# A fused gated cross-attention and ternary feed-forward layer: opening reordered, loads split over two queues, unread matmuls at more waits

## The reference

```python
def reference(x, ctx, g_xattn, g_ffn, Wk, Wv, bv, Wq, bq, Wo, bo, w1, conv_w, conv_b, w2):
    # x [8, 100, 512], ctx [8, 722, 512], Wq/Wk/Wv/Wo [512, 512], w1 [2048, 512], w2 [512, 2048]
    q = layernorm(x) @ Wq.T + bq
    k, v = ctx @ Wk.T, ctx @ Wv.T + bv
    p = softmax(q @ k.T / sqrt(512))
    x = x + tanh(g_xattn[0]) * ((p @ v) @ Wo.T + bo)
    # feed-forward: rows quantised to int8 steps, weights to -1, 0, 1 times their mean magnitude
    h = quant_rows(layernorm(x)) @ ternary(w1).T
    h = silu(conv1d over the 100 positions, 3 taps per hidden channel, + conv_b)
    return x + tanh(g_ffn[0]) * (quant_rows(h) @ ternary(w2).T)
```

## Time and profile before

| | us |
|---|---|
| median of 3 runs | 359.85 (353.22, 359.85, 360.3) |
| the profiled execution | 355.76 |
| its span | 353.9 |
| TensorE busy in the span | 293.7 (83%) |
| VectorE, ScalarE, GpSimd busy | 184.7, 154.0, 99.5 |
| mean granted TensorE clock | 0.923 of 2.4 GHz |

### The profile page before, as it was taken

One profiled execution on the slowest core, in us unless ns is written; L12 is line 12 of the kernel. 1 busy time (PEld: TensorE's weight loads), 2 busy tenths in 40 slices (PEclk: granted clock), 3 DMA queues, 4 the chain that ended last, 5 costly groups with the idle time before them and its releaser, 6 DMA issues.

```text
span 353.9 us, 4349 instructions
## 1 busy us (share of the span) xinstructions
PE 293.7 (83%) x1565; PEld 206.8 (58%) x1565; DVE 184.7 (52%) x390; ACT 154.0 (44%) x255; POOL 99.5 (28%) x96
## 2 busy tenths in 40 slices
PE   4957999989988989758988996776978897868695
PEld 2427899656536766537767784544836854434342
DVE  0094232330225127577577347489857545897562
ACT  3003228684367552588541234198731102976000
POOL 1008000024210980234214003053420802544070
PEclk9995599999999999985999998799988589999899
DMA  6998139806696259500240600000000000000002
GB/s 194 235 247 342 53 110 272 192 1 154 159 417 152 60 119 252 142 0 3 74 95 5 164 2 0 0 3 23 2 23 0 0 0 25 1 24 25 0 0 69
DMA packets 27950, 32.19 MB, mean 91 GB/s; under 512 B 17865, under 2 KB 17865, under 8 KB 26778
## 3 DMA queue, kind: packets, MB, share of 16 engines
q1 hardware_dynamic: 27930, 31.93, 33.0%
HBM read 26.09 MB, written 1.64 MB: 78 GB/s over the span
## 4 chain that ended last, share of the span: by engine, by line
PE 22%; DVE 15%; issue 12%; ACT 6%; POOL 3%; DVEq 0%; POOLq 0%; ACTq 0%
PE pvb L592 4%; PE yb L667 3%; DVE a L1093 3%; DVE u L1086 3%; PE ff L641 2%; DVE acc_q L1098 2%; ACT z L823 2%; PE yb L462 2%; ACT ab L817 2%; PE tr L552 2%; PE yb L464 1%; PE yb L463 1%; PE tr L676 1%; PE yb L627 1%; PE sc L571 1%
## 5 line engine op out<-in xcount | busy, mean ns | idle before, releaser
L873 POOL TENSOR_TENSOR z<-a,ab 128x300 f32<-128x300 f32 (+1 forms) x48 | 34.4, 716 | 67.7 <-DVE a L1093 67.7
L592 PE MATMUL pvb<-pt,ctx 120*128 120x100 f32 (+1 forms) x384 | 50.1, 293 | 1.8 <-ACT pt L754 1.8
L592 PEld LDWEIGHTS pvb<-pt,ctx 120*128 120x128 f32 (+1 forms) x384 | 49.0, 209 | 3.5 <-issue 3.4
L641 PE MATMUL ff<-xqt,w1t 128*128 128x300 bf16 (+1 forms) x192 | 30.4, 291 | 16.6 <-DVE u L1086 14.3
L571 PE MATMUL sc<-kt,qm 128*100 128x361 f32 x128 | 42.5, 481 | 0.0
L815 ACT ACTIVATE a<-u,convb,conv 128x300 f32<-128x300 f32 (+1 forms) x48 | 28.9, 602 | 15.5 <-DVE u L1086 15.2
L641 PEld LDWEIGHTS ff<-xqt,w1t 128*128 128x128 bf16 x192 | 17.2, 103 | 27.3 <-DVE u L1086 21.6
L552 PE MATMUL tr<-ident,ctx 120*128 120x120 f32 (+1 forms) x192 | 29.4, 276 | 4.1 <-ACT kt L733 3.2
L990 DVE COPY kt<-tr 128x361 f32<-128x361 f32 x32 | 17.0, 533 | 27.9 <-PE tr L552 24.8
L1093 DVE SCALAR_TENSOR_TENSOR a<-u,conv,a 128x297 f32<-128x297 f32 (+1 forms) x48 | 30.4, 633 | 1.2 <-ACT a L815 0.9
L571 PEld LDWEIGHTS sc<-kt,qm 128*100 128x100 f32 x128 | 21.1, 170 | 16.6 <-issue 2.5
(11 more groups left out here) (158 smaller groups left out, 480.4 us busy)
## 6 DMA issues: line engine op xcount, KB each, us to landing
ctx<-in_ctx_dram SPq DMA_DIRECT2D x16, 720.0 KB
wraw<-in_L_ffn_w_dram SPq DMA_DIRECT2D x8, 1024.0 KB, 12.6
x_sb<-in_x_dram SPq DMA_DIRECT2D x2, 800.0 KB
out_dram<-x_sb SPq DMA_DIRECT2D x8, 200.0 KB
wq_sb<-in_L_xattn_Wq_dram SPq DMA_DIRECT2D x4, 256.0 KB, 4.4
wk_sb<-in_L_xattn_Wk_dram SPq DMA_DIRECT2D x4, 256.0 KB, 5.4
wv_sb<-in_L_xattn_Wv_dram SPq DMA_DIRECT2D x1, 1024.0 KB, 5.0
wo_sb<-in_L_xattn_Wo_dram SPq DMA_DIRECT2D x1, 1024.0 KB, 8.4
```

The lines of the kernel that those rows point to most:

```text
L592: mm = nc.tensor.matmul(pvb[:, k * S:(k + 1) * S], cx[b % NCTX][0:r, i, k * P:(k + 1) * P], pt[0:r, i, :], start=(i == 0), stop=(i == 5))
L641: mm = nc.tensor.matmul(ffb[j % 2][:, 0:w], w1t[:, j * DK + k, :], xqt[:, k, 0:w], start=(k == 0), stop=(k == DK - 1))
L873: nc.gpsimd.tensor_tensor(z[:, q, 0:w, i].rearrange("p (b s) -> p b s", b=nb), a1[:, n % NBUF, 0:w].rearrange("p (b s) -> p b s", b=nb), a ...
```

## The change

- The opening's order: `m` is cut into eight steps of two products' banks; x's first half is loaded ahead of the last two pairs of Wq and Wk; the layer norm of the first half and transposes 0 to 3 run between those products. The statistics (`stat`) and the normalisation (`ln1`) are steps of their own. The split of M is two steps (`split`). Transposes 4 to 7 stand between the first scores, and tiles qt 4 to 7 in `fill`, in the banks ff0 and ff1.
- `bqk`: VectorE forms the sum over k of Wk times the bias in four operations (`bqp`), TensorE multiplies four times by one column of ones. `bvo`: VectorE sums Wo' times the bias in five operations, TensorE needs one product.
- GpSimd's normalisation of batches 4 to 7 takes a scale and a shift in place of a mean and a scale.
- x is loaded as 96 and 4 rows. The small loads (gates, biases, convolution) go to ScalarE's queue, ahead of its steps. ctx 1 is asked for in the opening, Wo ahead of Wv, w2's quarters between the turns of w1.
- The sums of w1 come later in the order, those of w2 between the `m2` steps; `FILL_CUTS` follow.
- `keep_up(bank, count)` issues unread matmuls into the bank of a step, behind its claim and ahead of its other waits: 2 for each `xqt`, 4 for each `rbc` and `am2`, 1 for each `ff` tile, 6 for each `am1`. A `busy` step of 4 is added ahead of `pt` of the last batch; the ones of 28 and 9 in the tail become 24 and 5. `keep_up` waits for all of w2 to be turned.

```diff
-FILL_CUTS = [17, 22, 33, 50, 60, 77, 89, 92]
+FILL_CUTS = [23, 28, 39, 56, 66, 83, 95, 98]
...
-    steps = [("gate",), ("ln1", 0), ("ln1", 1), ("m",), ("xt", 0), ("xt", 1), ("bqk",), ("xt", 2), ("xt", 3), ("xt", 4)]
-    for n in range(DK):
-        steps += [("qt", n)] + ([("xt", 5 + n)] if n < 3 else [])
-    steps += [("kt", 0, 0), ("kt", 0, 1)]
-    for n in range(DK):
-        steps += [("qt", DK + n)] + ([("kt", 0, 2 * n + 2), ("kt", 0, 2 * n + 3)] if n < 3 else []) + [("wsum", 0, n)]
-
-    fill = [("wot", k) for k in range(DK)] + [("wmean", 0), ("wi", 0, 0), ("m2", 0), ("wi", 0, 1), ("m2", 1)]
-    fill += [("wi", 0, 2), ("m2", 2), ("wi", 0, 3), ("m2", 3), ("bvo",)]
-    fill += [("wsum", 1, c) for c in range(CHUNK)] + [("wmean", 1)] + [("wi", 1, c) for c in range(CHUNK)]
+    steps = [("gate",), ("bqp", 0), ("bqp", 1), ("m", 0, 0), ("m", 0, 1), ("m", 1, 0), ("m", 1, 1), ("stat", 0), ("ln1", 0)]
+    steps += [("bqp", 2), ("m", 2, 0), ("m", 2, 1), ("xt", 0), ("xt", 1), ("m", 3, 0), ("split", 0), ("xt", 2), ("xt", 3)]
+    steps += [("m", 3, 1), ("split", 1), ("bqp", 3), ("qt", 0), ("bqk",), ("stat", 1), ("qt", 1), ("kt", 0, 0), ("kt", 0, 1)]
+    steps += [("ln1", 1), ("qt", 2), ("kt", 0, 2), ("kt", 0, 3), ("qt", 3), ("wsum", 0, 0), ("kt", 0, 4), ("kt", 0, 5)]
+    steps += [("kt", 0, 6), ("kt", 0, 7), ("scores", 0, 0), ("xt", 4), ("scores", 0, 1), ("xt", 5), ("wsum", 0, 1)]
+    steps += [("scores", 0, 2), ("xt", 6), ("scores", 0, 3), ("xt", 7)]
+
+    fill = [("qt", 4), ("wsum", 0, 2), ("qt", 5), ("wsum", 0, 3), ("qt", 6), ("wmean", 0), ("wi", 0, 0), ("qt", 7)]
+    fill += [("wot", 0), ("wot", 1), ("wi", 0, 1), ("wot", 2), ("wot", 3), ("wi", 0, 2), ("m2", 0), ("wi", 0, 3)]
+    fill += [("m2", 1), ("wsum", 1, 0), ("m2", 2), ("wsum", 1, 1), ("wsum", 1, 2), ("m2", 3), ("bvo",), ("wsum", 1, 3)]
+    fill += [("wmean", 1)] + [("wi", 1, c) for c in range(CHUNK)]
...
+        if b + 1 == B:
+            main += [("busy", 4)]
...
-    steps += [("busy", 10)] + norm[3:4] + [("busy", 4)] + norm[4:] + ff_f2(last, second[TAIL_F2:]) + [("busy", 28)]
-    steps += qz(last)[:1] + [("busy", 9)] + qz(last)[1:2] + [("busy", 18)] + qz(last)[2:] + [("f2 all", last)]
+    steps += [("busy", 10)] + norm[3:4] + [("busy", 4)] + norm[4:] + ff_f2(last, second[TAIL_F2:]) + [("busy", 24)]
+    steps += qz(last)[:1] + [("busy", 5)] + qz(last)[1:2] + [("busy", 18)] + qz(last)[2:] + [("f2 all", last)]
...
+        qt_bank = wide + [ffb[n % 2][:, :] for n in range(DK)]
...
-            sp.dma_start(rows1[0:1, D:D + 1], g_xattn.rearrange("(a b) -> a b", a=1)).then_inc(ld_gate, 16)
-            sp.dma_start(rows1[0:1, D + 1:D + 2], g_ffn.rearrange("(a b) -> a b", a=1)).then_inc(ld_gate, 16)
-            for k in range(DK):
+            def load_wqk(k):
                 sp.dma_start(wq_sb[:, k, :], wq.rearrange("(p k) d -> p k d", p=P)[:, k, :]).then_inc(ld_wqk[k], 16)
                 sp.dma_start(wk_sb[:, k, :], wk.rearrange("(p k) d -> p k d", p=P)[:, k, :]).then_inc(ld_wqk[k], 16)
-            for half in range(2):
+
+            def load_x(half):
+
                 bs = slice(half * B // 2, (half + 1) * B // 2)
-                sp.dma_start(x_sb[:, bs, :], x[bs].rearrange("b s d -> s b d")).then_inc(ld_x[half], 16)
-            sp.dma_start(biases[:, 0, :], bq.rearrange("(p k) -> p k", p=P)).then_inc(ld_bias, 16)
+                rows = x[bs].rearrange("b s d -> s b d")
+                sp.dma_start(x_sb[0:96, bs, :], rows[0:96]).then_inc(ld_x[half], 16)
+                sp.dma_start(x_sb[96:S, bs, :], rows[96:S]).then_inc(ld_x[half], 16)
+
+            load_wqk(0)
+            load_wqk(1)
+            load_x(0)
+            load_wqk(2)
+            load_wqk(3)
+            load_x(1)
             load_ctx(0)
-            sp.dma_start(biases[:, 1, :], bv.rearrange("(p k) -> p k", p=P)).then_inc(ld_bias, 16)
-            sp.dma_start(rows1[0:1, 0:D], bo.rearrange("(a b) -> a b", a=1)).then_inc(ld_bias, 16)
-            sp.dma_start(conv[:, :, :], conv_w.rearrange("(p j) o t -> p j (o t)", p=P)).then_inc(ld_bias, 16)
-            sp.dma_start(convb[:, :], conv_b.rearrange("(p j) -> p j", p=P)).then_inc(ld_bias, 16)
             for c in range(CHUNK):
                 load_w(0, c)
+            load_ctx(1)
 
             sp.wait_ge(xt_ps, B)
+            sp.dma_start(wo_sb[:, :, :], wo.rearrange("(m p) e -> p m e", p=P)).then_inc(ld_wo, 16)
             sp.dma_start(wv_sb[:, :, :], wv.rearrange("(p k) d -> p k d", p=P)).then_inc(ld_wv, 16)
-            sp.dma_start(wo_sb[:, :, :], wo.rearrange("(m p) e -> p m e", p=P)).then_inc(ld_wo, 16)
-            load_ctx(1)
+
+
+            sp.wait_ge(qt_ps, 2 * DK)
+            turn_w(0, 0)
+            turn_w(0, 1)
+            sp.wait_ge(w1t_ok[0], 16)
+            load_w(1, 0)
+            turn_w(0, 2)
+            sp.wait_ge(w1t_ok[1], 16)
+            load_w(1, 1)
             load_ctx(2)
-            for c in range(CHUNK):
-                turn_w(0, c)
-            for c in range(CHUNK):
-
-                sp.wait_ge(w1t_ok[c], 16)
-                load_w(1, c)
+            turn_w(0, 3)
+            sp.wait_ge(w1t_ok[2], 16)
+            load_w(1, 2)
+            sp.wait_ge(w1t_ok[3], 16)
+            load_w(1, 3)
             sp.wait_ge(pv_ps, DK)
...
+            def keep_up(bank, count):
+
+                pe.wait_ge(w2t_ok, 16 * CHUNK)
+                for _ in range(count):
+                    nc.tensor.matmul(bank[:, :], ident_bf[:, :], w2t[:, 0, :], start=True, stop=True)
...
-                    pe.wait_ge(ld_bias, 80)
+                    pe.wait_ge(bq_part_ok, DK)
                     claim("ff0", bqk_ok, 1)
                     for n in range(DK):
-                        for k in range(DK):
-                            mm = nc.tensor.matmul(ffb[0][:, n:n + 1], wk_sb[:, k, n * P:(n + 1) * P],
-                                                  biases[:, 0, k:k + 1], start=(k == 0), stop=(k == DK - 1))
+                        mm = nc.tensor.matmul(ffb[0][:, n:n + 1], bq_part[:, n * P:(n + 1) * P], ones[:, 0:1],
...
-                    pe.wait_ge(bvw_ok, DK)
-                    for k in range(DK):
-                        nc.tensor.matmul(ffb[0][0:S, :], bv_wide[:, k, :], wot[:, k, :], start=(k == 0), stop=False)
-                    nc.tensor.matmul(ffb[0][0:S, :], ones[0:1, 0:S], rows1[0:1, 0:D],
-                                     start=False, stop=True).then_inc(bvo_ps, 1)
+                    pe.wait_ge(bv_part_ok, 1)
+                    nc.tensor.matmul(ffb[0][0:S, :], ones[:, 0:S], bv_part[:, :], start=True, stop=True).then_inc(bvo_ps, 1)
...
                     claim("y", xqt_ok, b + 1)
+                    keep_up(yb, 2)
                     pe.wait_ge(xq_ok, b + 1)
...
                     n_bc += 1
+                    keep_up(yb, 4)
                     pe.wait_ge(diag_ok, n_bc)
...
                             pe.wait_ge(w1t_ok[c], 16)
+                    keep_up(ffb[j % 2], 1)
                     for k in range(DK):
...
                     claim("y", hmax_ok, g + 1)
+                    keep_up(yb, 6)
                     pe.wait_ge(acc_ok, (NJ // QUAD - 1) * (g + 1))
...
+                if kind == "bqp":
+                    k = step[1]
+                    dve.wait_ge(ld_wqk[k], 32)
+                    if k == 0:
+                        dve.wait_ge(ld_bq, 16)
+                        nc.vector.tensor_scalar(bq_part[:, :], wk_sb[:, 0, :], biases[:, 0, 0:1], None,
+                                                ALU.mult).then_inc(bq_part_ok, 1)
+                        continue
+
+                    dve.wait_ge(bq_part_ok, k)
+                    nc.vector.scalar_tensor_tensor(bq_part[:, :], wk_sb[:, k, :], biases[:, 0, k:k + 1], bq_part[:, :],
+                                                   ALU.mult, ALU.add).then_inc(bq_part_ok, 1)
...
+                        nc.vector.scalar_tensor_tensor(shift1[:, bs], mv[:, bs, 0], -1.0, rstd1[:, bs],
+                                                       ALU.mult, ALU.mult).then_inc(shift_ok, 1)
...
+                        dve.wait_ge(wot_ok, DK)
+                        dve.wait_ge(qt_ps, 2 * DK)
+                        dve.wait_ge(ld_bv, 16)
+                        dve.wait_ge(ld_bo, 16)
+                        link(nc.vector.tensor_scalar(bv_part[:, :], wot[:, 0, :], biases[:, 1, 0:1], None, ALU.mult))
+                        for k in range(1, DK):
+                            link(nc.vector.scalar_tensor_tensor(bv_part[:, :], wot[:, k, :], biases[:, 1, k:k + 1],
+                                                                bv_part[:, :], ALU.mult, ALU.add))
+                        nc.vector.tensor_tensor(bv_part[0:1, :], bv_part[0:1, :], rows1[0:1, 0:D],
+                                                ALU.add).then_inc(bv_part_ok, 1)
```

93 lines of the change are left out of this document (54 added, 39 removed).

## The result

| | before | after |
|---|---|---|
| runs, us | 353.22, 356.79, 359.85, 360.3 | 341.17, 341.29, 341.48, 342.03 |
| median | 358.32 | 341.38 |
| profiled execution | 355.76 | 341.29 |
| its span | 353.9 | 339.5 |
| mean granted TensorE clock | 0.923 | 0.975 |

The ratio of the two is 0.960, with an interval of 0.9525 to 0.9675: the change makes the kernel 4% faster. (Ratios here leave out runs more than 1.5% above the fastest of their kernel; medians take all.) The profiled executions differ by 14.5 us. The forecast was 340.0.

The account below looks back on a forecast made before the run. It saw an opening waiting on loads and VectorE, then TensorE's order as path, then TensorE in attention and VectorE and ScalarE in feed-forward. Gains of 18.2 - 10.0 + 7.8 = 16.0 us from 355.76 gave 339.8, said as 340; range 333 to 350.

Parts of the forecast that it names:

- The opening: Start up to the first qt tile: x at 12.5, qt at 25.0 instead of 38.89, 13.9 us earlier.
- the landmark: Transpose of batch 2 that waits for a kt copy, at 106.86 before; forecast 18.2 us earlier, near 89.
- the last term of that sum: SP's queue: w2's chunks come a few us early, halving TensorE's 2.12 us wait for a kt copy: +1.0.
- rival 4: w2 is late: group 0's first unread matmul waits 4 us for w2 to be turned; 344 us, chance 0.06.
- the five places: Half-clock stretches: group 0's ff and pv, y of batch 5, eight scores records, pv and y of batch 7; together 12.7 us.
- 7.8 less 10.0: Unread matmuls: 7.8 us expected back from a held clock, against a cost of 10.0 us on the path.
- One sign that I had named: Profile after: TensorE's busy time up by about 102 times 0.22 us less 12.
- 1 (the clock doesn't listen): Unread matmuls are pure work and don't hold TensorE's clock: 349 us, chance 0.18.
- 2 (loads bind): Opening: x and the third weight pair come as late as before, qt 5 to 6 us later: 345, chance 0.13.
- My sentence that TensorE would not use an earlier x: x in 96 + 4 rows comes 1 to 2 us sooner, unused by TensorE, which is in the product.
- 3 (the clock holds everywhere and w2 is quicker, 335): TensorE's clock holds everywhere and w2's path is quicker: 335 us, chance 0.17.
- 5: Slower than before: unread matmuls keep TensorE the bound at the lower clock; 381 us, chance 0.03.

Follow-up runs that it names:

- (4): Changed kernel with w2's third sum moved behind the last Wv product in ScalarE's order, transfers unchanged: 340.17 us.
- (3): Changed kernel with ctx 2 asked for ahead of the four turns of w1: 337.33 us, ratio 0.9383.
- (5): Changed kernel with ctx 2 first, then all four turns of w1, then w2's four loads: 334.64 us, ratio 0.9453.
- (8): Changed kernel with twelve more unread matmuls ahead of the claim of group 0's tenth ff tile: 340.76 us.
- run 1: Changed kernel without its unread matmuls at xqt, rbc, am1, am2 and ff, with the busy steps of the kernel before: 345.65 us.
- (2): Changed kernel without the 48 single unread matmuls ahead of the ff tiles: 341.56 us.
- run 9: Changed kernel with each half of x loaded as one copy of 100 rows instead of 96 and 4: 348.8 us.
- run 11: Changed kernel with the transfer order of (5) and the twelve unread matmuls of (8) together: 333.19 us, ratio 0.9444.

## Why the prediction was right, and where it was off

*The opening.* Right, and a little short: qt started 15.4 us earlier, forecast 13.9. The opening's own variation covers the difference (qt at 23.29 to 25.16 in ten profiles, forecast 25.0). x came at 11.96 (12.5), the product at 4.76 (4.8), the split's wait was 1.46. The first tile gave back 1.87 (1.9), the bias product took 0.95 (0.9 to 1.75). The product of `bvo` fell to 1.02 us (1.1). Up to the first kt unit of batch 2, one step ahead of the landmark, all terms but the last make 17.2 us, and 18.15 were measured.

*The step that failed* is the last term of that sum, "with chunks a few us early half of it goes: +1.0". It came as -5.2: the landmark gained 12.95 instead of 18.15. I took w2's chunks to come early since they are asked for early, and a turn between two loads to be as short as one alone. No row had shown a turn behind a load. The four turns of w1 before held the queue for 1.5 to 1.7 us each, and so did those in the row of 14.30 us, whose length is that of the waits for GpSimd's clips. Behind a load a turn holds the queue until the load's last packet is through; the third w2 quarter came at 89.19, and what was lost is the wait at 92.55 and the half clock behind it. Runs 3 to 5 show it: moving the reader moves the wait (4), moving one load moves the slow turn (3), taking the loads out from between the turns and ctx 2 ahead of them gives 6.5 us back (5). It is a third thing beside my rivals: rival 4 looked for late turns of w2 at 141.85, where nothing waited.

*The unread matmuls.* The mechanism was right, four of the five places held (y of batch 5, scores, pv and y of batch 7). Of the fifth, group 0, I had given half, and it stayed at 0.53 and 0.62, because the wait lies ahead of the claim (8). From pt of batch 1 on the change gains 2.0 us, where 7.8 less 10.0 is a loss of 2.2. Cut step by step, as in run 1, the changed kernel against the one before has 9.9 gained and 7.9 lost: the gain is 2.1 more than I had, since all four places held where I had given each 65%, and the cost is 2.1 less than 10.0. In run 1, with the same opening, the cost is 7.1. The 48 of the ff tiles, put at 1.3 + 1.2 + 1.0 us, cost 2.8 (2). The others, put at 6.5, cost 4 to 5, most of it at the xqt and broadcasts of groups 0 and 2 and at the new busy step; it is the six ahead of each am1 and the four ahead of group 1's broadcast that stood in waits.

One sign that I had named didn't come: TensorE's busy time was to go up by 10, and it went down by 2.8 (293.7 to 290.9). I had left out what the new opening and the two small products save. Run 1 has 282.4: 11.3 less by the new order, and 8.5 more by the unread matmuls.

The two errors, -6.2 (the term that came as -5.2 for +1.0) and +4.2 (from pt of batch 1 on), go far to cancel each other: the profiled execution gained 14.5 us where 16.0 was forecast, nearer than the terms were, and the forecast of 340.0 owes some of its closeness to that, which is luck.

*The rivals.* 1 (the clock doesn't listen) fell by run 1. 2 (loads bind) fell at 11.96, though run 9 shows it near: with x as one load TensorE is bound by loads after all, behind qt. My sentence that TensorE would not use an earlier x was wrong for that reason; the later loads use it. 3 (the clock holds everywhere and w2 is quicker, 335) didn't come by itself; two further edits bring it, in run 11 (333). 4 and 5 didn't come.
